# Post-norm decoder layer on one core: the PE projection of two heads one slot earlier, and a pair's value product split into eight and five key tiles

## The reference, cut to what matters

```python
C_q = Q @ Wq_d
C_kv = K @ Wkv_d
CqWqk = (C_q @ W_qk).reshape(b, n, H, LKV)
scores = jnp.einsum('bnhl,bkl->bhnk', CqWqk, C_kv) / jnp.sqrt(LKV)
attn = jax.nn.softmax(scores, axis=-1)
V_up = (C_kv @ Wv_u).reshape(b, nkv, H, HD)
out = jnp.einsum('bhnk,bkhd->bnhd', attn, V_up)
```

## Time and profile before

| | us |
|---|---|
| median of three runs | 2862.83 |
| lowest, highest | 2859.35, 2862.97 |
| the profiled execution | 2854.49 |
| its span, first to last instruction | 2852.5 |
| attention, first score to last value product | 390.5 to 1530 of the span |

### The profile page before, as it was taken

One profiled execution on the slowest core, in us unless ns is written; L12 is line 12 of the kernel. 1 busy time (PEld: TensorE's weight loads), 2 busy tenths in 40 slices (PEclk: granted clock), 3 DMA queues, 4 the chain that ended last, 5 costly groups with the idle time before them and its releaser, 6 DMA issues. The chain is left out here.

```text
span 2852.5 us, 41197 instructions
## 1 busy us (share of the span) xinstructions
PE 2636.4 (92%) x14360; PEld 1988.6 (70%) x14360; DVE 2264.6 (79%) x2125; ACT 1671.3 (59%) x2611; POOL 1941.2 (68%) x1423
## 2 busy tenths in 40 slices
PE   6867889999999999999996999999999999999997
PEld 3645566666666666666664788888888888788885
DVE  1436568888887788878884799999999899899988
ACT  2242467777777777777775545444545555555553
POOL 1000247767777777767874888888887788888883
PEclk9979999999999999999998999999999999999999
DMA  7304566767777777677765132222222322232221
GB/s 263 120 31 171 170 227 201 222 194 207 216 216 213 226 215 220 199 235 243 226 200 186 55 108 96 74 74 74 74 67 91 109 75 89 74 116 77 74 96 74
DMA packets 166768, 420.60 MB, mean 147 GB/s; under 512 B 30113, under 2 KB 57634, under 8 KB 166050
## 3 DMA queue, kind: packets, MB, share of 16 engines
q1 hardware_dynamic: 161698, 407.93, 45.7%
q10 hardware_dynamic: 4864, 10.03, 0.9%
HBM read 248.43 MB, written 75.04 MB: 113 GB/s over the span
## 5 line engine op out<-in xcount | busy, mean ns | idle before, releaser
L1566 DVE SCALAR_TENSOR_TENSOR c_acc<-c_ps,c_sd,c_acc 128x1024 f32<-128x1024 f32 x448 | 573.2, 1282 | 97.0 <-PE c_ps L1422 96.9
L1160 POOL COPY b_pt<-b_tn 32x640 f32<-32x640 f32 x640 | 457.6, 715 | 262.6 <-DVE b_tn L1068 231.0
L1477 ACT ACTIVATE c_scaled<-c_ps,c_sgu 128x1024 f32<-128x1024 f32 x336 | 375.6, 1118 | 425.0 <-PE c_ps L1422 422.5
L1062 DVE TENSOR_REDUCE b_nm<-b_sc 128x1 f32<-128x1604 f32 x256 | 468.1, 1828 | 189.4 <-PE b_sc L899 188.2
L981 ACT ACTIVATE b_pr<-b_sc,b_nm 128x799 f32<-128x799 f32 (+1 forms) x512 | 476.9, 934 | 237.3 <-DVE b_nm L1062 214.7
L1649 POOL TENSOR_TENSOR c_sum_u<-c_sum_u,c_scaled 128x1024 f32<-128x1024 f32 x168 | 404.9, 2410 | 116.0 <-ACT c_scaled L1477 115.5
L1649 POOL TENSOR_TENSOR c_sum_g<-c_sum_g,c_scaled 128x1024 f32<-128x1024 f32 x168 | 405.0, 2411 | 82.5 <-ACT c_scaled L1477 82.4
L899 PE MATMUL b_sc<-b_kh,b_qs 128*128 128x402 f32 (+1 forms) x1024 | 403.3, 394 | 41.2 <-ACT b_pr L981 37.5
L918 PE MATMUL b_po<-b_pt,shared 128*64 128x256 f32 x2560 | 389.4, 392 | 29.5 <-DMA b_pt<-b_tn 29.1
L1068 DVE STREAM_TRANSPOSE b_tn<-b_pr 128x1280 f32<-128x1280 f32 x256 | 384.7, 1503 | 3.3 <-ACT b_pr L981 2.0
L899 PE MATMUL b_sc<-b_kl,b_qs 128*128 128x402 f32 (+1 forms) x1024 | 357.3, 349 | 0.0
(11 more groups left out here) (192 smaller groups left out, 4371.6 us busy)
## 6 DMA issues: line engine op xcount, KB each, us to landing
b_pt<-b_tn SPq DMA_DIRECT2D x1152, 80.0 KB, 2.7
c_uw_int<-wint_u SPq DMA_DIRECT2D x56, 512.0 KB, 3.4
c_gw_int<-wint_g SPq DMA_DIRECT2D x56, 512.0 KB, 3.4
c_dw_int<-wint_d SPq DMA_DIRECT2D x56, 512.0 KB, 3.4
a_cx<-in_b_ctxT SPq DMA_DIRECT2D x16, 1608.0 KB, 11.1
b_rw<-in_c_gw SPq DMA_DIRECT2D x28, 512.0 KB, 4.1
b_rz<-in_c_gz SPq DMA_DIRECT2D x28, 512.0 KB, 5.6
b_rw<-in_c_uw SPq DMA_DIRECT2D x28, 512.0 KB, 4.0
```

The source lines that it names most:

```text
L1062: V.tensor_reduce(nm[:, u % 2:u % 2 + 1], both, AXY, ALU.max, negate=True).then_inc(s_nm, 1)
L1160: G.tensor_copy(pt[s][32 * c:32 * c + 32, a, :, :], tn[s][32 * a:32 * a + 32, c, :, :]).then_inc(s_block, 1)
L1477: S.activation(dst[:, :], pair[SLOT[x, t] % 4][:, :], ACT.Identity, scale=scale(x, t)).then_inc(s_e, 1)
L1566: V.scalar_tensor_tensor(out=total, in0=pair[SLOT[x, t] % 4][:, :], scalar=scale(x, t), in1=total, op0=ALU.mult, op1=ALU.add).then_inc(s_a ...
```

## The change

The projection of two heads moves from slot 5 to slot 4, on all engines and in the bank's order, and slot 4 becomes a special slot in the place of slot 5. The value product takes tiles 0 to 7 in the odd slot and 8 to 12 in the even one.

```diff
@@ def ring_events():
-        if k % 8 == 5 and k + 3 < NU:
-            out.append(("project", (k + 3) // 4, 0))
+        if k % 8 == 4 and k + 4 < NU:
+            out.append(("project", (k + 4) // 4, 0))
@@ def special(k):
-    return k in CN_AT or k % 8 == 5 and k + 3 < NU or k % 4 == OUT_AT % 4 and k >= OUT_AT
+    return k in CN_AT or k % 8 == 4 and k + 4 < NU or k % 4 == OUT_AT % 4 and k >= OUT_AT
@@ tensor(), weigh
-                for t in (range(0, 7), range(7, NKT))[part]:
+                for t in (range(0, 8), range(8, NKT))[part]:
@@ tensor(), scalar() and vector(), the loop over k
-                if k % 8 == 5 and k + 3 < NU:
-                    project((k + 3) // 4)
+                if k % 8 == 4 and k + 4 < NU:
+                    project((k + 4) // 4)
```

## The result

The changed kernel took 2882.02 us in the median of six runs (2871.51 to 2887.03), the kernel before 2863.21 us beside it: a ratio of 1.0060, 95% interval 1.0041 to 1.0080. By the ratios that is 17, 10 and 13 us more, in the mean 0.47% or 13 us. The profiled execution has a span of 2872.1 us against 2852.5.

The account below looks back on a forecast made before the run. It took a 4.06 us loop through DVE, ACT and PE as the bound, with DVE's own 4.84 us in slot 5. Terms 0 + 0 - 4.6 + 4.1 + 13 = +12 us gave 2875 us, range 2852 to 2889.

Parts of the forecast that it names:

- The split: Value product, eight and five tiles for seven and six: 1.87 and 1.44 us again, 0 us.
- Slots 4 and 5, "nothing": Projection moved: slot 4 becomes DVE's 4.84 us, slot 5 the loop's 4.06; sum 8.90 against 8.91, nothing.
- Slot 6: Slot 6 falls from 4.44 to 4.29 us, 0.15 us 31 times: -4.6 us (0 to -5).
- The norm pieces: Six layer norm pieces on DVE in a slot 4, no longer hidden: 0.65 + 0.04 us each, +4.1 us.
- The exchange: Slot 4's transposed pair is ready 1.55 us later, so PE waits more for the DMAs: +13 us (0 to +28).
- PE's waits in slot 1: Slot 6's pair starts its exchange late: 0.5 us for 24 pairs, +12 us; a wait in slot 7 gives back 6.
- The pair of slot 7: Pair transposed by slot 4, multiplied in slot 7: ready later, less time for its exchange, +5 us of waits.
- The waits in slot 3: The pair behind slot 6's pair may start its exchange late too: +2 us.
- slot 4 at 4.84: Sign: slot 4 takes 4.84 us from maximum to maximum, 5.5 where a norm piece stands in it.
- waits of over 40 us: Sign: PE's waits for the exchange rise from 29 us to over 40, most in slots 7 and 1.
- The rival that filling PE's hole is what counts: PE's 4.48 us binds slot 4, not DVE: 11.5 us saved, with slot 6 16, about 2848; chance 0.18.
- The rival that the DMAs keep up: Exchange landings come early enough, no new waits: -0.5 us, up to 5 either way, 2862; chance 0.30.

Follow-up runs that it names:

- the two variants of it on another chip: Against the changed kernel: value product kept at seven and six tiles, 2877.91 us (1.0053); norm pieces of slots 20 and 28 put into 21 and 29, 2873.50 us (1.0039).
- The two profiles with early blocks: Changed kernel with ACT's two exchange blocks ahead of slot 3's first exponential, not at the slot's end, run twice: 2869.70 us (1.0029) and 2867.85 us (1.0022).

## Why the prediction was right, and where it was not

The forecast of +12 us is met by the measured +13 (+17, +10 and +13 in three comparisons). That the number fits so well is luck: the sum lacks one term of 9 us and holds another that is too large by about 7. With only one of the two put right it would have been +21 or +5.

- **The split** was right: 1.88 and 1.44 us, ratio 0.9999 alone.
- **Slots 4 and 5, "nothing"**, failed, at the sentence that ACT's casts are within ACT's idle time. DVE's bound of 4.84 us was right and is seen when ACT's blocks are moved. But ACT's idle time in slot 4 comes too late: its two blocks of slot 3, 1.47 us, stand ahead of the casts, and slot 4 is 5.31 us, or 5.06 behind a slot 3 that was lengthened. Only behind the long slots 3, those with a latent transpose above all, does it keep 4.87, because there ACT finishes first. That is 9 us in all (162.6 against 153.6) that the sum lacked.
- **Slot 6** was right: 4.28 us for 4.44, -5.0 us over the 31 slots.
- **The norm pieces** cost 0.57 us each where 0.69 was reckoned, 3.4 us in all.
- **The exchange** was mis-sized: +13 forecast, about +6 by the mean of five profiles, with a spread that allows 3 to 9. The mechanism stood in part: of the 32 pairs of slot 6, 15 to 22 start 0.5 us late or more, where 4 or 5 did, and the forecast had 24. What was too dear is the 0.5 us of wait for each of them: PE's waits in slot 1 rose from 11 to 14 us (means of two and of five profiles), where the forecast had +12, less 6 for a wait ahead of them. The pair of slot 7 was to wait 5 us more. It is ready 10.3 us after its predecessor now, where it was 8.4 (means over 32 pairs), and SP has issued its nine DMAs 6.1 us after it is ready, where it took 6.9; its waits rose by 2 us. The waits in slot 3 rose by 2 us, the forecast's size.

In the sum as measured, 9 + 3.4 - 5.0 + 6 = 13 us, the last term is the soft one. Of the signs that the prediction named, slot 5, slot 6 and the two products came out; slot 4 at 4.84 didn't, and waits of over 40 us were not seen in the changed kernel itself (33.7, 29.4 and 38.5), only in the two variants of it on another chip. The two profiles with early blocks have 44.3 and 42.8 us, but the variants with late blocks have 42.2 and 40.8, so the runs don't tell whether ACT's delay in slot 4 gives the exchanges room.

One reading of the trace before needs a word: slots 1 and 3 take 4.06 us in the median, as the prediction says, but 4.43 and 4.41 in the mean, because waits for the exchange and latent transposes lengthen some of them. It is these longer slots 3 that shorten the slot 4 behind them.

The rival that filling PE's hole is what counts is out: DVE's 4.84 binds in slot 4, over the 4.6 at which it would have decided, PE's waits for ACT fell by 12 of 64, and the time rose. The rival that the DMAs keep up is not right either, since the waits rose, but for this term the measured +6 lies about as near to its 0 as to the forecast's 13.

## What to carry to other kernels

When work is moved one slot, write out for every engine that takes part in it what stands just ahead of it in the new place; a busy share or a total of idle time doesn't say whether the idle time lies before or behind. Here the idle time of PE was of no use, since DVE's part of the same step filled its slot and ACT's part stood behind an exchange. And before an order is changed to fill an idle engine, look for work on the loop's other engines that can go ahead of the wait: two blocks of ACT placed in its idle time, with one DMA fewer, gave 0.55% in the changed order and 0.48% in the old one.

## What the runs showed that was not expected

Executions of one kernel differ in their waits for the exchange by up to 9 us (29.4 and 38.5 us in two profiles of the changed kernel), and five profiles with the same place of the projection and of ACT's blocks range from 29.4 to 42.2. A gain or loss of under some 10 us in these waits can't be read from one profile. Taking one of nine DMAs away cut these waits from 29.1 to 7.5 us, more than the 11% of its traffic; in that run slots 0, 2 and 4 were longer too, which leaves each exchange more time, and how much of the fall is due to that was not tested.
